# Windowed attention and depthwise mixing on one core: the order of ScalarE's and TensorE's steps in a strip is changed

## The reference, cut to what matters

```python
x = layernorm2d(x0, ln_w, ln_b)                 # over the 96 channels
q, k = split(conv1x1(x, qk_w, qk_b))            # 48 + 48 channels
vs = conv1x1(x, vs_w, vs_b)                     # 96 channels
local = depthwise_conv3x3(vs, depth_w) + depth_b
yw = softmax(qw @ kw.T * SCALE) @ vw            # in shifted windows, first 48 channels
y = concat([yw, v2])                            # v2: the other 48 channels of vs
s = (y + local).mean(axis=(2, 3))
ca = sigmoid(fu2_w @ leaky_relu(fu1_w @ s, 0.2))
y = y * ca + local * (1.0 - ca)                 # gate, needs the whole image
z = conv1x1(y, proj_w, proj_b) + x0
```

## Time and profile before

| | us |
|---|---|
| median of 3 runs | 1436.88 |
| lowest, highest | 1436.03, 1438.45 |
| the profiled execution | 1438.88 |
| its span | 1437.2 |
| TensorE busy | 1303.7 (91%) |
| VectorE busy | 1177.0 (82%) |
| ScalarE busy | 957.3 (67%) |
| GpSimd busy | 410.8 (29%) |
| granted TensorE clock, mean | 0.984 |

### The profile page before, as it was taken

One profiled execution on the slowest core, in us unless ns is written; L12 is line 12 of the kernel. 1 busy time (PEld: TensorE's weight loads), 2 busy tenths in 40 slices (PEclk: granted clock), 3 DMA queues, 4 the chain that ended last, 5 costly groups with the idle time before them and its releaser, 6 DMA issues.

```text
span 1437.2 us, 38309 instructions
## 1 busy us (share of the span) xinstructions
PE 1303.7 (91%) x12403; PEld 780.7 (54%) x12403; DVE 1177.0 (82%) x2028; ACT 957.3 (67%) x2375; POOL 410.8 (29%) x870
## 2 busy tenths in 40 slices
PE   5999999899999999999999999899999999579995
PEld 3676766655555555555555555555555555323331
DVE  3565665588989989999898998898898999778996
ACT  2567676777777777777777777777777777533342
POOL 3122121124323443224323443233234433110110
PEclk9999999999999999999999999999999999889998
DMA  2122222546655676566656675566566665568995
GB/s 65 57 77 74 68 85 63 138 103 168 153 152 143 163 173 148 143 151 173 150 148 144 168 162 145 133 173 147 148 146 168 163 150 150 131 153 194 228 224 136
DMA packets 81364, 203.13 MB, mean 141 GB/s; under 512 B 15248, under 2 KB 19112, under 8 KB 81320
## 3 DMA queue, kind: packets, MB, share of 16 engines
q1 hardware_dynamic: 72424, 176.65, 47.7%
q0 software_dynamic: 7168, 25.17, 9.5%
q10 hardware_dynamic: 1728, 0.79, 0.2%
HBM read 136.57 MB, written 64.91 MB: 140 GB/s over the span
## 4 chain that ended last, share of the span: by engine, by line
PE 48%; DMA 27%; ACT 10%; DVE 7%; issue 6%; SPq 1%; POOLq 1%; ACTq 0%; POOL 0%; DVEq 0%
DMA zs<-in_x 22%; PE banks_g L652 6%; PE banks_s L557 5%; PE banks_g L645 5%; PE banks_g L532 4%; PE banks_g L540 4%; DVE mx L1085 4%; PE banks_g L647 4%; PE banks_t L565 4%; DMA ycat<-y_img 4%; ACT zs L891 3%; ACT oo L901 3%; PE banks_t L645 3%; PE banks_a L546 3%; PE banks_t L519 2%
## 5 line engine op out<-in xcount | busy, mean ns | idle before, releaser
L1259 DVE SCALAR_TENSOR_TENSOR mixed<-vin,c_pack,mixed 96x1024 f32<-96x1024 f32 x352 | 451.0, 1281 | 8.5 <-ACT mixed L880 1.5
L1271 DVE SCALAR_TENSOR_TENSOR oo<-zs,l_w,oo 96x1016 f32<-96x1016 f32 x192 | 243.9, 1270 | 48.8 <-ACT oo L901 44.6
L447 POOL COPY vrow<-vw 96x16 f32<-96x16 f32 (+2 forms) x520 | 267.4, 569 | 0.0
L467 POOL TENSOR_TENSOR rest<-rest 96x1 f32<-96x1 f32 x64 | 51.9, 811 | 627.6 <-ACT zs L891 627.6
L1057 DVE BATCH_NORM_STATS2 bn<-banks_a 128x6 f32<-128x96 f32 x528 | 99.8, 251 | 100.3 <-PE banks_a L507 98.9
L1085 DVE TENSOR_REDUCE mx<-banks_s 128x16 f32<-128x1024 f32 x130 | 158.4, 1219 | 25.5 <-PE banks_s L557 24.9
L557 PE MATMUL banks_s<-km,qd 64*128 64x128 f32 x2080 | 152.0, 285 | 25.5 <-issue 22.6
L854 ACT ACTIVATE pt<-banks_t 128x512 f32<-128x512 f32 x256 | 138.4, 592 | 45.7 <-PE banks_t L565 45.4
L901 ACT ACTIVATE oo<-zs,c_pack,l_w 96x1024 f32<-96x1024 f32 x64 | 79.4, 1241 | 132.6 <-DMA zs<-in_x 124.4
L645 PE MATMUL banks_g<-vin,proj_t 128*96 128x512 f32 (+1 forms) x288 | 152.9, 632 | 12.5 <-DMA ycat<-y_img 5.1
L557 PEld LDWEIGHTS banks_s<-km,qd 64*128 64x128 f32 x2080 | 128.8, 188 | 50.7 <-issue 48.1
(11 more groups left out here) (151 smaller groups left out, 1815.2 us busy)
## 6 DMA issues: line engine op xcount, KB each, us to landing
vin<-v_img SPq DMA_DIRECT2D x64, 495.0 KB, 5.7
v_img<-vrow SPq DMA_DIRECT2D x130, 198.0 KB, 2.5
xc<-in_x SPq DMA_DIRECT2D x134, 192.0 KB, 7.2
zs<-in_x POOLq DMA_DIRECT2D x64, 384.0 KB, 9.1
out<-oo SPq DMA_DIRECT2D x64, 384.0 KB, 3.5
y_img<-ybuf SPq DMA_DIRECT2D x128, 99.0 KB, 2.0
ycat<-v_img SPq DMA_DIRECT2D x64, 198.0 KB, 4.9
ycat<-y_img SPq DMA_DIRECT2D x64, 198.0 KB, 8.0
```

Of the source, the lines that this page charges most:

```text
L447: nc.gpsimd.tensor_copy(dst.rearrange("c r (p x) -> c p r x", x=min(WS, src.shape[-1])), src).then_inc(vrow_done, 1)
L1259: v.scalar_tensor_tensor(out=mb[:C, par, :, 0:W], in0=vin[:C, par, 1 + dh:1 + dh + WS, 1 + dw:1 + dw + W], scalar=depth_w[:, DVE_TAPS[m]:D ...
L1271: v.scalar_tensor_tensor(out=oo[:, par, :, to], in0=zs[:, par, 1 + dh:1 + dh + WS, of], scalar=l1_w[:, tap:tap + 1], in1=oo[:, par, :, to] ...
```

## The change

Only the order of steps changes, in strips with attention and mixing.

- TensorE: `project` is split into `project_taps` (waits for the loads, tap matmul) and `project_rows`. In a plain strip the taps of half 0 stand ahead of the waits for queries and maxima and of scores 0, behind the wait for the keys; those of half 1 stand between values 1 and max_transposed. The rows stay where they were. In the gated strip the taps stay beside the rows.
- ScalarE: `first` stands directly behind the queries (and behind `projections` in the gated strip), ahead of tap0; the two `sum_x` stand behind maxima_out, ahead of values.

```diff
--- before.py
+++ after.py
@@ -634,7 +634,7 @@
             def z_bank(par, last):
                 return banks_t if last and par == 1 else banks_g
 
-            def project(u, um, par, c, last):
+            def project_taps(u, um, par, c, last):
                 z = z_bank(par, last)[:C, c, :]
                 pe.wait_ge(vin_loaded[par], 16 * (um + 1))
                 pe.wait_ge(ycat_loaded[par], 80 * (um + 1))
@@ -644,7 +644,13 @@
                     rows = 128 if n == 0 else C
                     mm(z, proj_t[:rows, n, :], vin[:rows, par, at:at + 4, 1 + dw:1 + dw + W],
                        start=n == 0, stop=False)
-                mm(z, proj_c[:], ycat[:, par, 4 * c:4 * c + 4, 0:W], start=False, stop=False)
+
+            def project_rows(par, c, last):
+                mm(z_bank(par, last)[:C, c, :], proj_c[:], ycat[:, par, 4 * c:4 * c + 4, 0:W], start=False, stop=False)
+
+            def project(u, um, par, c, last):
+                project_taps(u, um, par, c, last)
+                project_rows(par, c, last)
 
             def project_mixed(u, par, last):
                 pe.wait_ge(m_step, mixes(u + 1, last))
@@ -715,18 +721,21 @@
                     rstd_rows(t + 2, 0)
                     rstd_rows(t + 2, 1)
                     pe.wait_ge(km_done, 2 * (t + 2))
-                    pe.wait_ge(qd_done, 2 * (t + 2))
-                    pe.wait_ge(nmx_done, t + 1)
                 if gated is not None:
                     pe.wait_ge(mid_act, gated + 1)
                     if not attend:
                         pe.wait_ge(y1_done, YO * B * NS)
-                if attend:
+                if cur and gated is None:
+                    project_taps(u, um, par, 0, tail)
+                if attend:
+                    pe.wait_ge(qd_done, 2 * (t + 2))
+                    pe.wait_ge(nmx_done, t + 1)
                     scores(1 - k, 0)
                 if gated is not None:
                     pe.wait_ge(proj_done, N_PROJ * (gated + 1) - 2)
+                    project_taps(u, um, par, 0, tail)
                 if cur:
-                    project(u, um, par, 0, tail)
+                    project_rows(par, 0, tail)
                 if gate is not None and not attend:
                     one_column(gate, fu1T[:], st[:, 5:6], 1, R, 1)
                 if attend:
@@ -735,13 +744,17 @@
                     pe.wait_ge(mx_done, 2 * (t + 1) + 1)
                     scores(1 - k, 1)
                     values(t, k, 1)
+                if cur and gated is None:
+                    project_taps(u, um, par, 1, tail)
+                if attend:
                     pe.wait_ge(yq_done, FREE + 2 * t + 1)
                     max_transposed(t + 1)
                 if gated is not None:
                     one_column(gated, projT[:], st[:, 12:13], 3, C, 3)
                     one_column(gated, projT[:], st[:, 13:14], 4, C, 3)
+                    project_taps(u, um, par, 1, tail)
                 if cur:
-                    project(u, um, par, 1, tail)
+                    project_rows(par, 1, tail)
                 if gate is not None and not attend:
                     one_column(gate, fu2T[:], tr[:, 1:2], 2, C, 2)
                 if gated is not None:
@@ -982,6 +995,8 @@
                     queries(t + 1, 1 - k)
                     if gated is not None:
                         projections(gated, u)
+                if ahead and attend:
+                    first(u + 1, h - NS // 2, k)
                 if prev and not late:
                     tap0(u - 1, h - NS // 2 - 1, k, after)
                     if gated is None:
@@ -989,19 +1004,18 @@
                 if late and after is None:
                     tap0(u - 2, h - NS // 2 - 2 + k, 1 - k, before)
                     halo(u - 1, k)
-                if attend:
-                    sum_x(t + 2, k, h + 1, 0)
-                    sum_x(t + 2, k, h + 1, 1)
                 if gate is not None:
                     image_sums(gate)
                 if attend:
                     y_out(t - 1, 1 - k, h - 1 + k)
                 if gate is not None:
                     rows_sum(gate)
-                if ahead:
+                if ahead and not attend:
                     first(u + 1, h - NS // 2, k)
                 if attend:
                     maxima_out(t + 1, 1 - k)
+                    sum_x(t + 2, k, h + 1, 0)
+                    sum_x(t + 2, k, h + 1, 1)
                 if attend:
                     values(t + 1, 1 - k)
                 elif gate is not None:
```

## The result

The changed kernel took 1418.0 us (median of 4 runs, 1412.05 to 1421.52) against 1437.66 for the kernel before, now also of 4 runs; the ratio is 0.985, with a 95% interval of 0.981 to 0.990. A second comparison, among the experiments, gave 0.984 (0.981 to 0.987). The profiled execution took 1415.28 us, its span was 1413.6. Forecast were 1415 for the median and 1416.4 for the profiled execution. One execution of TensorE's part alone, among the experiments, took 2151 us at a granted clock of 0.56 and is left out of that kernel's median.

What follows compares the result with a forecast made beforehand. Each strip was bounded by the larger of two cycles, 10.70 + DMA or TensorE's 19.85. Plain strips 20.5 plus gates 2 gave 22.5 off 1438.9: 1416.4, then 1414.4 for the median, said as 1415; range 1402 to 1432.

Steps and rivals of the forecast that it cites:

- The strip: Plain strip, from one transposition of the maxima (anchor) to the next: both limits fall by 0.50, mean 20.1 to 19.6 us.
- What of the 0.93 arrives: Second-half taps on TensorE, 0.93 us, move ahead of the anchor; only about 0.5 arrives at ScalarE's copy of z.
- the wait of 0.76 at a gate: ScalarE's values copy waited 0.76 us after the maxima's copy at an image's gate; taken as its DMA issue holding ScalarE.
- The rival in which ScalarE isn't delayed: Chance 0.12: the DMA issue doesn't hold ScalarE, the whole 0.93 arrives, some 0.8 us a strip, time 1402.
- The landing: DMA adding into zs: starts 0.5 us earlier relative to SyncE's loads, yet keeps its time, 0 growth.
- The tied landing: Chance 0.15: the addition starts 0.5 us earlier but lands when SyncE's loads are served; DMA grows by 0.5, time 1432.
- Vin: Load that first on ScalarE needs: lands by 817.9, before the queries end at 819.06, so first's cost is nil.
- The slower rival: Chance 0.07: late vin holds the second convolution's first tap; at 10.2 us each strip loses 1.0, wins 0.5, time 1458.
- First half, 0.51: First-half taps on TensorE fill the wait ahead of the first scores: gain 0.51 us, with the later scores staying hidden.
- the 13.84 forecast: TensorE from the values' projection to the next anchor: 13.79 - 0.51 - 0.37 + 0.93 = 13.84 us, strip 19.35.
- VectorE's sum of 19.15: VectorE's strip: busy 18.2 us plus an estimated 0.9 of signals and waits, some 19.15, close behind the other limits.
- Gates: Three gated intervals: 1.2 us gained by earlier maxima copies, 0.6 lost at the first tap, net 2; interval behind each, none.

Runs made afterwards that it cites:

- the sums in the wait: Changed kernel with the two sums of x moved between first and the first tap, into ScalarE's wait for the DMA; 1413.8 us, ratio 0.975.

## Why the prediction was right, point by point

- **The strip.** Forecast 19.6 from 20.1; measured 19.60 from 20.13. The plain strips gave 41 x 0.53 = 21.8 us, forecast 20.5.
- **What of the 0.93 arrives.** Forecast: the mixed passes end at + 3.67, the copy of z starts at + 4.17, since the DMA issue holds ScalarE and the sums stand ahead of the values copies. Measured: + 3.65, and + 4.18 in the mean. Inside this sum the DMA issue was taken too short, from the wait of 0.76 at a gate: it is 0.87 in a plain strip, so the values copies start at + 2.77, not + 2.63. The rounding up from 4.1 to 4.17 hid this. The rival in which ScalarE isn't delayed falls by the 0.87 between the maxima's copy and the sums.
- **The landing.** It was to stay at 9.3 although it starts earlier. Changed kernel, time to landing of the addition (L468): the median is 9.0, against 9.2. The tied landing, which needed 0.5 more, falls:

```profile
DMA to landing us min/median/max: 7.8/9.0/10.0
```

With the sums ahead of the output copies, where the addition starts 0.24 earlier still, it is about the same:

```profile
DMA to landing us min/median/max: 7.8/9.1/10.2
```

- **Vin.** *first* had no idle time before it in any strip of this stage. The slower rival falls.
- **First half, 0.51.** This term was about twice too large. The gap ahead of the first scores is filled, as forecast, but I called the later scores hidden behind VectorE, and TensorE waits there for the first maxima, 0.23 on its matmuls. From the values' projection to the anchor the shortest plain strips took 13.76 before and 13.49 with the first half's taps alone: 0.27 gained. With both halves they took 13.98, against the 13.84 forecast. So strips with early landings take 19.3 to 19.5, not 19.35. What bounds them is TensorE together with that wait, not VectorE's sum of 19.15: with the sums of x ahead of the output copies and the same work on VectorE, strips of 19.00 occur, so 19.15 was no limit.
- **Gates.** This term failed. Forecast was a net gain of 2 us, measured 0.5: the three gated intervals took 22.52, 21.99 and 22.12 (from 22.67, 22.75, 22.91; 1.7 less), but the interval behind each, which I put at nothing, took 21.76, 21.34 and 21.34 (from 20.97, 21.12, 21.11; 1.2 more). In the last two the stretch from the values' projection to the anchor took 14.02 instead of 13.79. It holds 0.93 of second-half taps, of which 0.37 fill the wait at the anchor, and gains only 0.27 from the first half: 14.08 by this sum, where the forecast had 13.84. For the first, 0.8 longer, the cause stays open; the kernel with the sums ahead of the output copies had 21.20 in one profile and 21.75 in the other, so it isn't the order alone. The gain in the gated intervals was credited to ScalarE's part, and that too fails: ScalarE's part alone left the second and third at 22.81 and 22.78, and TensorE's part alone had 21.91 and 21.82 for the second and 21.71 for the third in the profile without a fall of the clock there.
- **What I didn't price.** I worked out each part against the kernel before, but never ScalarE's part beside TensorE's alone. The sum in my own text would have shown it: *first* takes 1.15 off ScalarE's way to the values copies, the sums put 1.22 there. The forecast was right for the two parts together, and silent on one of them costing time beside the other.

The measured median was 3 above the forecast; the profiled execution was 1.1 below its own. That the latter came so close is in part luck: the plain strips gave 1.3 more than forecast, the gates 1.5 less, and the stages outside gave 1.3 that weren't forecast. Executions of the changed kernel differ by up to 10 us (1412.05 to 1421.52), those of others by more (1432.65 to 1448.44 for the first half's taps alone). A cause of some 4 to 5 is named below; the rest stays open.

## What to carry to other kernels

When two cycles through one strip are nearly equal, price both: filling the gap of one is worth nothing until the other is shortened, and the two together give more than the sum of each alone (here 0.53 against 0.00 + 0.36). When a producer's work is moved earlier, sum the consumer's list up to the point where it takes it; the shift arrives only down to that sum, and a piece moved out of one wait must not land between two links of the chain. A change that moves work on two engines should be priced for each engine's part beside the other, since one part can cost what the other earns. Use a long wait for pieces that nothing near needs, and leave them out of iterations in which that wait doesn't exist.

## What the runs showed of the hardware

**A DMA issue on ScalarE holds it.** Copy, issue and next instruction follow as 797.37, 797.67 and 798.51: from the copy's end 0.87, of which 0.64 is the issue. It is so in 38 strips, 31.9 us in all (0.84 on average):

```profile
ACT x_junk L808 <- ACT nmx L860: 31.9, 38, 0.9
```

**TensorE's clock in the first gate strip.** There TensorE waits for the late maxima and their DMA, whose issue takes 1.24 here; in the changed kernel:

```profile
278.74 1.24 ACTq L862 DMA_DIRECT2D qd<-nmx  x1
...
280.89 2.08 PE L565 MATMUL banks_t<-qd,km 64*128 64x128 f32 x16 [1.37 <-DMA qd<-nmx]
```

The granted clock falls from its full 2.4 GHz to 1.2 GHz (0.50 in the rows below), and these 16 passes take 2.08 us instead of 1.16. How long it stays there differs. Busy times by stretch (columns as in the earlier trace rows) of the changed kernel:

```profile
278.00:281.00 3.00, 1.49 (x15) 1.15 (x15) 2.69 (x16) 1.23 (x4) 0.00 (x0) 0.87 0.36 83
281.00:290.00 9.00, 8.03 (x48) 4.90 (x52) 5.00 (x13) 5.54 (x16) 2.40 (x9) 0.66 0.94 209
290.00:300.00 10.00, 9.05 (x124) 5.96 (x118) 7.75 (x16) 8.68 (x24) 1.14 (x3) 1.00 0.14 42
```

And of the kernel with the sums ahead of the output copies, first profile:

```profile
278.00:281.00 3.00, 1.08 (x10) 0.87 (x10) 2.79 (x11) 1.58 (x6) 0.00 (x0) 0.69 0.29 73
281.00:290.00 9.00, 9.00 (x48) 5.55 (x49) 4.40 (x13) 3.61 (x9) 2.79 (x9) 0.50 0.95 213
290.00:300.00 10.00, 10.00 (x74) 5.98 (x67) 6.99 (x15) 8.55 (x21) 0.75 (x3) 0.52 0.14 42
```

In the 3 us in which the fall lies TensorE was busy 1.49 and 1.08 us. The first interval took 22.5 us, the second 26.9. TensorE's part alone had 26.9 in one profile and 22.6 in the other, so it is spread and not a property of one order. The place differs too: in the profiles of ScalarE's part alone and of the sums in the wait the clock fell one strip earlier (that interval took 19.6 and 19.8 us instead of 16.6, at a granted clock of 0.83), and the second profile of the sums ahead of the output copies had 0.59 from 921 to 931, in a third gated interval of 25.4 us instead of 22.3. Whether an order with a shorter wait at the gate meets it less often, these few profiles don't settle.
